# An expert layer with routed rows on one core: a weight rounding moved to the block ahead, and gathers moved ahead of scatters at the end of the loop

## The reference, cut to what matters

```python
def _L0_cond_ref(Efou, y, weight):                    # 32 x 256 x 256
    ys = y * scale
    d = rsqrt(einsum('bi,io->bo', ys * ys, weight * weight) + EPS)
    return einsum('bsi,io->bso', Efou * ys[:, None, :], weight) * d[:, None, :]

def _L0_ffn_ref(input_emb, W1, b1, W2, b2, Wr, br):   # E = 8 experts, D = 256, H = 1024
    logits = einsum('bsd,de->bse', input_emb, Wr) + br
    route_w = softmax(logits); mask = the two best of 8
    routed = route_w * mask, normed to a sum of 1
    h = relu(einsum('bsd,edh->ebsh', input_emb, W1) + b1)
    expert_out = einsum('ebsh,ehd->ebsd', h, W2) + b2
    return einsum('bse,ebsd->bsd', routed, expert_out)

x + _L0_ffn_ref(_L0_cond_ref(x, cond, weight), ...)
```

## Time and profile before

| | us |
|---|---|
| median of 3 runs | 867.27 (867.22 to 867.81) |
| the profiled execution | 867.41 |
| its span | 865.6 |
| granted clock, mean | 0.994 |
| PE busy | 838.5 |
| DVE busy | 739.9 |
| ACT busy | 566.0 |
| POOL busy | 464.0 |
| start of block 38 (r_cur, L1496) | 749.06 |
| start of block 40 | 773.65 |

### The profile page before, as it was taken

How to read it: one execution, slowest core, us unless ns; L and a number is a source line. 1 busy time by engine, 2 the same in 40 slices (tenths; PEclk the granted TensorE clock), 3 DMA queues, 4 the chain that set the end, 5 groups by cost and what they waited for, 6 DMA issues and landing times.

```text
span 865.6 us, 19224 instructions
## 1 busy us (share of the span) xinstructions
PE 838.5 (97%) x5616; PEld 798.6 (92%) x5616; DVE 739.9 (85%) x1483; ACT 566.0 (65%) x1022; POOL 464.0 (54%) x424
## 2 busy tenths in 40 slices
PE   5997999999999999999999999999999999999996
PEld 5985999999999999999999999999999999999995
DVE  3795888899989888988898888888888888888994
ACT  5786666788777665565556555655565556688783
POOL 6984453554434445455545554555455545555653
PEclk9998999999999999999999999999999999999999
DMA  7896837786353453425442544253343524774872
GB/s 232 305 322 230 272 78 214 195 251 172 81 142 81 84 133 89 113 42 121 102 113 42 120 103 113 41 121 76 92 89 51 148 43 89 183 217 121 218 206 26
DMA packets 55001, 118.38 MB, mean 137 GB/s; under 512 B 7312, under 2 KB 33328, under 8 KB 54320
## 3 DMA queue, kind: packets, MB, share of 16 engines
q1 hardware_dynamic: 25040, 69.48, 24.7%
q0 software_dynamic: 25536, 35.69, 24.2%
q10 hardware_dynamic: 4384, 12.71, 4.3%
HBM read 91.07 MB, written 35.17 MB: 146 GB/s over the span
## 4 chain that ended last, share of the span: by engine, by line
PE 85%; DVE 7%; ACT 4%; issue 3%; ACTq 1%; DMA 1%; POOL 0%; SPq 0%; POOLq 0%; DVEq 0%
PE psum L1746 14%; PE psum L1730 14%; PE psum L1732 13%; PE psum L1731 13%; PE psum L1745 7%; PE psum L1747 5%; PE psum L1749 5%; PE psum L1748 5%; PE psum L1743 2%; PE psum L1702 2%; ACT w_parts L813 2%; DVE w_parts L1441 2%; PE psum L1744 1%; PE psum L1612 1%; PE psum L1613 1%
## 5 line engine op out<-in xcount | busy, mean ns | idle before, releaser
L886 ACT ACTIVATE h<-psum,b_all 128x384 f32<-128x384 f32 (+1 forms) x376 | 209.2, 560 | 211.1 <-PE psum L1732 172.0
L1730 PE MATMUL psum<-z_hi,w_parts 128*128 128x384 f32 (+1 forms) x752 | 251.3, 334 | 4.4 <-DVE w_parts L1441 3.5
L1441 DVE TENSOR_TENSOR w_parts<-raw,w_parts 128x1024 fp32r<-128x1024 f32 x188 | 229.7, 1222 | 24.0 <-ACT w_parts L813 22.5
L1732 PE MATMUL psum<-z_hi,w_parts 128*128 128x384 f32 (+1 forms) x752 | 245.0, 326 | 0.0
L1731 PE MATMUL psum<-z_lo,w_parts 128*128 128x384 f32 (+1 forms) x752 | 245.0, 326 | 0.0
L1521 DVE TENSOR_TENSOR h_lo<-h,h_hi 128x384 fp32r<-128x384 f32 (+1 forms) x376 | 200.2, 533 | 22.6 <-ACT h L886 8.0
L813 ACT ACTIVATE w_parts<-raw 128x1024 fp32r<-128x1024 f32 x188 | 198.7, 1058 | 12.7 <-PE psum L1746 10.4
L673 POOL DMA_INDIRECT out<-y,idx_put x91 | 168.6, 1853 | 46.2 <-POOL idx_put L669 25.0
L1746 PE MATMUL psum<-w_parts,h_hi 128*128 128x512 f32 x525 | 188.7, 394 | 0.0
L1730 PEld LDWEIGHTS psum<-z_hi,w_parts 128*128 128x128 f32 x752 | 141.3, 188 | 10.4 <-issue 5.5
L1745 PE MATMUL psum<-w_parts,h_lo 128*128 128x256 f32 x525 | 146.6, 279 | 0.0
(11 more groups left out here) (249 smaller groups left out, 1136.0 us busy)
## 6 DMA issues: line engine op xcount, KB each, us to landing
raw<-in_experts SPq DMA_DIRECT2D x96, 512.0 KB
x_buf<-in_xT SPq DMA_DIRECT2D x12, 512.0 KB, 8.6
z_rows<-z_all ACTq DMA_DIRECT2D x2, 2112.0 KB, 9.8
d_rep<-d_rows SPq DMA_DIRECT2D x3, 1056.0 KB, 7.0
z_rows<-z_all SPq DMA_DIRECT2D x1, 2112.0 KB, 12.6
z_rows<-z_once SPq DMA_DIRECT2D x1, 2112.0 KB, 14.8
raw<-in_xT SPq DMA_DIRECT2D x4, 512.0 KB, 9.5
out<-y,idx_put POOLq DMA_INDIRECT x91
```

What stands on the lines that cost most here:

```text
L886: act.activation(h[c % NHP][:, 0:width], h_ps[c % n_h][:, 0:width], ACT.Relu, bias=b1_all[:, ds(e, 1), c]).then_inc(s_relu, 1)
L1441: dve.tensor_tensor(out=w_lo[k][:], in0=raw[k][:], in1=w_hi[k][:].bitcast(f32), op=ALU.subtract).then_inc(s_wlo, 1)
L1730: pe.matmul(hp, w1(w_hi, c, dc), z_hi[:, dc, 0:width], start=(dc == 0), stop=False)
L1732: ins = pe.matmul(hp, w1(w_lo, c, dc), z_hi[:, dc, 0:width], start=False, stop=(dc == DC - 1))
```

## The change

Three things change. From block 14 on, quarter 2 of block b is rounded at the end of block b-1, behind z_hi and (in the tail) quarter 1. The y of block 37 goes into y_other, the buffer that was the second y of the early blocks, so y of block 38 no longer waits for the scatter of block 37 but for that of block 36. And on GpSimd the gathers for blocks 39 and 40 both go ahead of the scatters of blocks 37 and 38; the tail's loop on GpSimd begins one block later. DVE's block 39 is written out of its loop so that it can have its own wait.

```diff
         def y_at(b):
+            if isinstance(b, int) and b == NA - 1:
+                return y_other
             return y[b % 2] if isinstance(b, int) and b < N1 - 1 else y[0]
...
-                        in_=y[0][:, q, :], in_offset=None, compute_op=ALU.add).then_inc(s_put, 16)
+                        in_=y_at(b)[:, q, :], in_offset=None, compute_op=ALU.add).then_inc(s_put, 16)
...
-            row_free(NA)
-            gather(NA + 1, True)
+            for b in (NA, NA + 1):
+                row_free(b)
+                gather(b + 1, True)
             y_ready(NA - 1)
             scatter_add(NA - 1)
+            y_ready(NA, True)
+            scatter_add(NA, True)
             last = last_of(pool)
-            with pool.Fori(NA + 1, last) as b:
+            with pool.Fori(NA + 2, last) as b:
...
-                    if c == 0:
+                    if c == 0 and isinstance(b, int) and b < N1:
                         weights_hi(b, 2, seg, fresh)
...
                 if wide:
                     weights_hi(b + 1, 1, seg_next, False)
+                if not (isinstance(b, int) and b < N1 - 1):
+                    weights_hi(b + 1, 2, seg_next, False)
...
-                if tail:
+                if tail and isinstance(b, int) and b == NA:
+                    dve.wait_ge(s_put, NA * (16 * Q))
+                elif tail:
                     dve.wait_ge(s_put, b * (16 * QB) + 16 * (Q + MOVED))
...
-                after_tail = tail and not isinstance(b, int)
+                after_tail = tail and not (isinstance(b, int) and b == NA)
...
             block_of_dve(NA, False, True)
+            block_of_dve(NA + 1, False, True)
             last_block = last_of(dve)
-            with dve.Fori(NA + 1, last_block) as b:
+            with dve.Fori(NA + 2, last_block) as b:
```

## The result

The changed kernel takes 871.78 us (median of 5 runs, 870.89 to 872.49) against 867.27 us before (867.07 to 868.54): a ratio of 1.0049 with a 95% interval of 1.0039 to 1.0060, so it is slower by half a percent. The forecast was 871.0, in a range from 867.9 to 872.9.

What follows compares the result with a forecast made beforehand. TensorE, busy for 97% of the span, was taken to bound the kernel, so only its idle time could be won. From 867.41 us, -3.2 + 5.1 + 1.9 = +3.8 gave 871.2, set to 871.0; range 867.9 to 872.9.

Steps and rivals of the forecast that it cites:

- The rounding, -3.2: Tail blocks: quarter 2 rounded earlier ends PE's wait for VectorE's subtraction, 0.35 us in each of nine blocks.
- The gather first, and scatter 37 behind it: GpSimd, loop's end: gather for 40 issued to 757.6, then scatter 37's three issues to 764.4.
- Landing of scatter 37: Loop's end: from its last issue's end to landed 3.2 us, at 767.6; bounds 2.35 and 4.8.
- Scatter 38: GpSimd, loop's end: first issue at 768.6, two issues taking 4.8 us, to 773.4.
- Its landing: Scatter 38 lands 3.2 us later, at 776.6; VectorE's y of block 39 stands 4.6 us for it.
- The gather for 41: GpSimd, behind scatter 38: lands at 780.1, PE wants it at 779.2; 0.5 us taken, up to 0.9.
- The clock, +1.9: PE behind the 4.6 us stall: granted clock falls to 0.50, costing 1.9 us, bounds 0 and 2.6.
- The loop's blocks: Three-tile loop blocks: the moved rounding gives nothing, since PE has no gap; they stay 17.32 us.
- the clock holds: Rival, 13%: block 39's stall comes, but PE's clock stays at 1.00; 869.2 us.
- short landings: Rival, 10%: loop's-end stall shrinks to 2.4 us and the clock holds; 866.5 us, no change.
- the stores are hidden: Rival, 10%: y of block 39 doesn't stand, as scatter 38 lands by 772.0; 864.1 us.
- A deeper stall: Rival, 7%, loop's end: loaded landings, issues slowed by VectorE's subtractions, and a late gather; 873.5 us and more.

Runs made afterwards that it cites:

- the other placing: Kernel before, with only quarter 2's rounding moved, to the start of the tail block's ScalarE work behind the register reads: 866.94 us, ratio 0.9979.
- order_only: Changed kernel with quarter 2's rounding back where it was; GpSimd's order, y_other and VectorE's wait kept: 875.24 us, ratio 1.0080.
- the four kernels with PE written out: Changed kernel, PE's blocks 38 to 40 written out, with 44, no, 68 and again no filling matmuls: 872.63, 874.33, 871.91, 873.54 us.
- y39_buffer: Changed kernel with y_other used for y of block 39 too, so that no y waits for the scatter ahead: 873.8 us, ratio 1.0075.
- the control: Changed kernel with PE's blocks 38 to 40 written out and no filling matmuls: 874.33 us, and 873.54 in a second pair.
- round_only: Kernel before, with only quarter 2's rounding moved to the end of the block ahead: 867.78 us, ratio 0.9990.
- old_order: Changed kernel, but GpSimd scatters block 37 ahead of the gather for block 40, as before: 868.6 us, ratio 0.9998.
- row_buffer: Kernel before, rounding behind register reads, early gather for 40 into a free row buffer, y of 37 in y_other, PE's 38 and 39 written out: 865.8 us, ratio 0.9977.

## Why the prediction held, step by step

- **The rounding, -3.2.** As sized. 0.50 in block 38, 0.33 in each of blocks 39 to 45, and 0.42 in the last stretch make 3.2. The sequencer's cost was real: 0.1 a block, by the earlier relu of the other placing.
- **The gather first, and scatter 37 behind it.** Counted from block 38's start (747.63 here, 749.06 before) the gather for 40 was over at 8.1 (I had 8.5), and scatter 37's last issue at 15.1 (15.3).
- **Landing of scatter 37**, 3.2 in my sum: 3.9 us from the end of its last issue. Nearer the middle of my bounds than the quiet row of 2.35, and far from the 0.5 that my weighing against it would have given. That quiet row is itself long for one, since its issue took 2.31; the kernel's last scatter, with an issue of 1.55, took 3.9 us from its start to its landing.
- **Scatter 38.** Errors that cancel. Between the copy and the first issue I had 0.8 and the row says 1.70, the wait that stood as 1.76 in the earlier trace rows and that I overlooked there. Its two issues took 3.4, where I had 4.8: the one subtraction near them (769.22 to 770.45) began behind the first issue and was all but over at the second, and then VectorE stood still. With the longer landing ahead of it, it ended at 24.3, as in my sum. That is luck.
- **Its landing**, 3.2: 3.76. The stall came to 5.3 on VectorE and 5.4 on PE, against 4.6. The same landing took only 2.3 to 2.5 in order_only and in the four kernels with PE written out, so 3.2 was inside its spread and no better founded than that.
- **The gather for 41**, 0.5: nothing in this kernel. It landed ahead of PE. The 5.1 of this step and the 5.3 measured agree partly because that surplus covered the short landings. That it is the next thing late, y39_buffer shows.
- **The clock, +1.9.** Right in kind, too small: 2.80. I had taken what twelve matmuls lost in 74 to 76 us, and here PE was at 0.50 from 777.93 to about 783.7, 5.8 us in which half of the work's time is lost. My upper bound was 2.6. The table by stretch of the changed kernel (length, busy PE, clock, DMA share, GB/s):

```profile
776.00:778.00 2.00, 0.07 (x1) 0.73 0.22 63
778.00:780.00 2.00, 2.00 (x11) 0.50 0.13 14
780.00:782.00 2.00, 2.00 (x11) 0.50 0.85 263
782.00:784.00 2.00, 2.00 (x12) 0.57 1.01 165
784.00:786.00 2.00, 2.00 (x19) 1.00 0.83 213
```

From 778 on PE is busy for the whole of these stretches and gets through 11 or 12 instructions in 2 us where it does 19 at 1.00.
- **The loop's blocks**: 17.32, as said.

In the tail -3.2 + 5.3 + 2.8 = +4.9, where I had +3.8. The medians differ by 4.5. The mechanism held, but that the size came so near owes something to chance: with PE's code written out, which moved the issues against VectorE's subtractions, the same stall was 7.6.

Of the rivals, *the clock holds* fell by the 0.50, *short landings* by the 3.9 and 3.76, and *the stores are hidden* by the 5.27 of y. *A deeper stall* fell by the time, but its slowed issues and its late gather are what made the control and y39_buffer slower still. The 864.1 of the hidden stores takes the rounding's 3.2 as if it stood by itself. In the old order it doesn't: round_only and old_order took 867.8 and 868.6 beside 868.45, because the shorter blocks bring the gather for 40 and scatter 37 onto the path. In the new order without a stall nobody measured it; the nearest is row_buffer, with a tail 3.5 us shorter. What I had not read is how little slack y and the gather for 40 had before for the rounding alone.

## What to carry to other kernels

When two stores and two loads share one queue of issues, putting a load ahead moves every store behind it, and a second buffer for the first store helps only the first: walk the queue to the last buffer that is used again, and think of giving the load a buffer of its own rather than a better place (row_buffer, whose lead on its neighbour in the time is within the noise). A gain in every iteration comes with a price where the slack is thinnest, here the two blocks at the change of shape; ask of each transfer there how late it may be once everything is faster. And when PE idles for some microseconds, take the price of the low clock from the rows of the work that follows and not from the gap's length: 2.8 us behind 5.4 of idleness, 1.5 behind 5.9 and an estimated 1.7 behind 7.6, by how much of the low stretch was left when PE came back.

## What the hardware showed unasked

**GpSimd's issue goes long beside VectorE's subtraction, and only beside one that runs already.** In eight of the traces, from the loop's end on, 168 scatter issues have a row. The 131 that began while the 128x1024 subtraction of the weights was running took, by the median, 1.55 us plus what the subtraction still had to run, less 0.09; they reach from 1.56 to 2.63. The 37 others took 1.55 by the median, and 33 of them no more than 1.64, also those beside which a subtraction began later: 768.53 with 1.55, though VectorE's L1448 started at 769.22. Rows above show it: 777.86 began 1.08 us ahead of the end of the subtraction of 777.72, and took 2.58. Issues of gathers take 0.95 to 1.24 and went to 1.78 to 2.03 in rows of six traces where a subtraction had just begun, and GpSimd's small copies of indices do the same, 0.18 us alone and 1.03 in y39_buffer. It is read from start times over many rows; no run was made for it alone. The Trainium skill (SBUF — State Buffer, "SBUF: two separate sides") has a port pair that VectorE and GpSimd hold by turns for a whole instruction: with two SBUF inputs a VectorE instruction takes part, against GpSimd instructions that read SBUF, and whoever starts first keeps it. The rows agree for the side of GpSimd. The other side doesn't show: subtractions that began during an issue took 1.21 to 1.23 us like the rest.

**A landing has no fixed price.** From the end of the issue to the landing of its 128 KB it took 2.1 to 2.6 us at the end of the kernels, where little else moves. At the loop's end scatter 37 took 3.5 to 4.8, and scatter 38 took 3.76 in the changed kernel and 2.3 to 2.5 in five others, as far as a wait shows them. What of that is the load of other queues stays open.
